# Routed experts: the inner layer handed over in two halves from two banks, and the biases asked for behind the first weights

## The chip, the cores and the metric

One Trainium2 chip, one core of it. The metric is the time of one execution on the device in microseconds (us). The kernel before took 3376.59 us as the median of three runs (3375.28 to 3383.07). PE is the matmul engine (PEld its weight loads), ACT, DVE and POOL are the scalar, vector and GpSimd engines, and SP issues DMAs. PSUM is the accumulator memory, eight banks of 512 float32 values in each of 128 partitions.

## The reference, cut to what matters

Two layers of a graph network, each a graph stage and then a feed-forward stage, over 2500 nodes of 1024 features. The change touches only the last part, the routed experts of the second feed-forward stage (D = 1024, H = 256, E = 8, two experts for each token):

```python
h1 = gelu(einsum('td,edh->teh', flat, rw1) + rb1[None], approximate=False)
expert_out = einsum('teh,ehd->ted', h1, rw2) + rb2[None]
mixed = einsum('ted,te->td', expert_out, weights)      # weights: the two top probabilities, else 0
return (shared_out + mixed).reshape(b, s, d)
```

## The kernel before, in words

The program is a row of stages. The last one, `stage_experts`, is the only one that changes. The stage before it sorts the (token, expert) pairs into 28 groups (PG) of 256 places (GT = 2 tiles of 128 tokens, q = 0 and 1), each group with one expert, and leaves the expert of each group and the token of each place in SBUF. Weights are read again for every group: `raw1` and `raw2` hold 1 MB each, the inner and the outer weights of one expert.

Every float32 product is made of three fast ones: each operand is split into a high part (a copy to the fast format, by ACT) and a low part (the operand less the high part, by DVE), and `split_products` sums high*high, high*low, low*high.

`in_turn(PG, body, 2)` writes the stage out as 30 bodies s = 0 to 29. In body s an engine serves group s (lag 0: loads and splits of weights), group s-1 (lag 1: tokens and inner layer) and group s-2 (lag 2: outer layer and output). Each engine runs its own list in order, and semaphores join the lists. For each body:

- SP (L1979 to L1988) waits until `raw1` has been used and asks for the next inner weights, then the same for `raw2`. Ahead of the loop it asks for the inner biases of all experts (`all_bias1`, two DMAs whose pieces are single values), and in the first turn, behind the weights, for the outer biases (`all_bias2`, 32 KB spread to all 128 partitions, 4 MB written).
- POOL gathers the rows of the two tiles of group s (L1999), and then scatters and adds the output rows of group s-2 into the output (L2009); a scatter waits for that of the group before to have landed.
- PE: transposes of tile 0 of group s-1 into `turned` (L2028, a buffer of two banks that both tiles use in turn), the outer product of tile 0 of group s-2 into `y` (12 matmuls of 512 columns), transposes of tile 1, outer product of tile 1, and then the inner product of group s-1 into `hidden` (48 matmuls of 256 columns: first the 24 of inner features 0 to 127, then the 24 of 128 to 255). Both halves of `hidden` lie in one bank, and one semaphore step says that both are done.
- ACT: copy `hi` of tile 0 and of tile 1 out of `turned` (L2058), high parts of the weights `w1_hi` (L2065) and `w2_hi` (L2068), a small copy of the bias (L2073), the Gelu of both halves of `hidden` (L2079, two instructions), and then the scaling of the two output tiles of group s-2 by their probabilities (L2086).
- DVE: `lo` of tile 0 (L2102), the outer bias added to `y` of tile 0 (L2113), the same for tile 1, low parts of both weights (L1479), and then `h_hi` (L2131) and `h_lo` (L1479) of both halves together.

Transposes of tile 1 wait until `lo` of tile 0 has been made, since they overwrite `turned`. ACT and DVE wait ahead of their first instruction of the stage until all three bias DMAs have landed (`small_in` at 48).

Of the kernel before, what the change touches and what calls it, by code (L numbers as in the profile page):

```python
# [11 lines left out]
P = 128  # L12
# [10 lines left out]
GT = 2  # L23
# [1925 lines left out]
def stage_experts(nc, g):  # L1949
    with ExitStack() as ctx:  # L1950
# [5 lines left out]
        all_bias1, bias1, all_bias2 = sb("all_bias1", [P, EXPERTS * 2]), sb("bias1", [P, 2, 2]), sb("all_bias2", [P, EXPERTS * D])  # L1956
        rows = sb("rows", [P, 2, GT, D])
        hi, lo = sb("hi", [P, KD, GT * P], F32R), sb("lo", [P, KD, GT * P], F32R)
        act_out = sb("act_out", [P, 2 * GT * P])
        h_hi, h_lo = sb("h_hi", [P, 2, GT * P], F32R), sb("h_lo", [P, 2, GT * P], F32R)  # L1960
        y_out = sb("y_out", [P, 2, GT, D])
        turned, y = a.psum("e_turned", [P, 2, HALF]), a.psum("e_y", [P, GT, 2, HALF])
        hidden = a.psum("e_hidden", [P, HALF])
        names = ("small_in raw1_in raw2_in raw1_used raw2_used w1_high w2_high v_done turned_ready "
                 "hi_ready lo_ready hidden_ready act_ready split_ready y_ready y_kept y_scaled bias1_ready").split()
        m = Named(**{n: a.sem(f"e_{n}") for n in names})
        gathered = [[a.sem(f"e_gathered{k}{q}") for q in range(GT)] for k in range(2)]
# [3 lines left out]

        @block.sync
        def _(sp):
            with nc.allow_non_contiguous_dma(reason="two thousand parameters"):
                for c in range(2):
                    sp.dma_start(all_bias1[:].rearrange("p (e m) -> p m e", m=2)[:, c, :],  # L1976
                                 g.rb1.rearrange("e (m p) -> m p e", p=P)[c]).then_inc(m.small_in, 16)

            for i in range(PG):  # L1979
                e = sp.value_load(g.expert[0:1, i:i + 1], min_val=0, max_val=EXPERTS - 1)  # L1980
                at_least(sp, m.raw1_used, i)
                sp.dma_start(raw1[:].rearrange("p (c f) -> p c f", c=KD),
                             g.rw1.rearrange("e (c p) f -> p (e c) f", p=P)[:, bass.ds(e * KD, KD), :]).then_inc(m.raw1_in, 16)
                at_least(sp, m.raw2_used, i)
                sp.dma_start(raw2[:].rearrange("p (m n) -> p m n", m=2),
                             g.rw2.rearrange("e (m p) n -> p (e m) n", p=P)[:, bass.ds(e * 2, 2), :]).then_inc(m.raw2_in, 16)
                if i == 0:
                    sp.dma_start(all_bias2[:], g.rb2.rearrange("e d -> (e d)").partition_broadcast(P)).then_inc(m.small_in, 16)  # L1988

        @block.gpsimd  # L1990
        def _(pool):
# [23 lines left out]
        @block.tensor  # L2015
        def _(pe):
            t = nc.tensor

            def body(item):
                for q in range(GT):  # L2020
                    it = item(1)
                    if it:
                        k = it.i % 2
                        n = it.i * GT + q
                        pe.wait_ge(gathered[k][q], (it.i // 2 + 1) * 16)
                        at_least(pe, m.lo_ready, n)
                        for c in range(KD):
                            tr = t.transpose(turned[:, c // 4, (c % 4) * P:(c % 4 + 1) * P],  # L2028
                                             rows[:, k, q, c * P:(c + 1) * P], g.ident[:])
                        tr.then_inc(m.turned_ready, 1)  # L2030
                    it = item(2)
                    if it:
                        k = it.i % 2
                        pe.wait_ge(m.split_ready, it.i + 1)
                        pe.wait_ge(m.raw2_used, it.i + 1)
                        at_least(pe, m.y_kept, it.i * GT + q - 1)
                        expert_output(t, y[:, q], h_hi, h_lo, w2_hi[:, k], w2_lo[:, k], q).then_inc(m.y_ready, 1)
                it = item(1)
                if it:
                    k = it.i % 2  # L2040
                    pe.wait_ge(m.lo_ready, (it.i + 1) * GT)
                    pe.wait_ge(m.raw1_used, it.i + 1)
                    at_least(pe, m.act_ready, it.i)
                    expert_hidden(t, hidden, w1_hi[:, k], w1_lo[:, k], hi, lo).then_inc(m.hidden_ready, 1)
            in_turn(PG, body, 2)

        @block.scalar
        def _(act):
            s = nc.scalar
            act.wait_ge(m.small_in, 48)  # L2050

            def body(item):
                for q in range(GT):
                    it = item(1)
                    if it:
                        act.wait_ge(m.turned_ready, it.i * GT + q + 1)
                        at_least(act, m.hidden_ready, it.i)
                        s.copy(hi[:, :, q * P:(q + 1) * P],  # L2058
                               turned[:].rearrange("p h (c n) -> p (h c) n", n=P)).then_inc(m.hi_ready, 1)
                it = item(0)  # L2060
                if it:
                    k = it.i % 2
                    act.wait_ge(m.raw1_in, (it.i + 1) * 16)
                    at_least(act, m.hidden_ready, it.i - 1)
# [5 lines left out]
                if it:  # L2070
                    k = it.i % 2
                    e = act.value_load(g.expert[0:1, it.i:it.i + 1], min_val=0, max_val=EXPERTS - 1)
                    s.copy(bias1[:, k, :], all_bias1[:, bass.ds(e * 2, 2)]).then_inc(m.bias1_ready, 1)  # L2073
                    act.wait_ge(m.hidden_ready, it.i + 1)
                    at_least(act, m.split_ready, it.i)
                    act.wait_ge(m.bias1_ready, it.i + 1)
                    for c in range(2):
                        cols = slice(c * GT * P, (c + 1) * GT * P)
                        ins = s.activation(act_out[:, cols], hidden[:, cols], ACT.Gelu, bias=bias1[:, k, c:c + 1])  # L2079
                    ins.then_inc(m.act_ready, 1)  # L2080
                it = item(2)
                if it:
                    for q in range(GT):
# [7 lines left out]
        def _(dve):  # L2091
            v = nc.vector
            st = Steps(dve, m.v_done)
            dve.wait_ge(m.small_in, 48)

            def body(item):
                for q in range(GT):
# [7 lines left out]
                    if it:  # L2105
                        k = it.i % 2
                        n = it.i * GT + q
                        if q == 0:
                            e = dve.value_load(g.expert[0:1, it.i:it.i + 1], min_val=0, max_val=EXPERTS - 1)
                            shift = all_bias2[:, bass.ds(e * D, D)]  # L2110
                        dve.wait_ge(m.y_ready, n + 1)
                        at_least(dve, y_added, (it.i - 1) * GT * 16)
# [3 lines left out]
                if it:  # L2116
# [2 lines left out]
                    dve.wait_ge(m.w1_high, it.i + 1)  # L2119
                    split_vector(v, w1_lo[:, k].rearrange("p c f -> p (c f)"), raw1[:],  # L2120
                                 w1_hi[:, k].rearrange("p c f -> p (c f)"), m.raw1_used)
                    dve.wait_ge(m.raw2_in, (it.i + 1) * 16)
                    dve.wait_ge(m.w2_high, it.i + 1)
                    split_vector(v, w2_lo[:, k].rearrange("p m n -> p (m n)"), raw2[:],
                                 w2_hi[:, k].rearrange("p m n -> p (m n)"), m.raw2_used)
                it = item(1)
                if it:
                    dve.wait_ge(m.act_ready, it.i + 1)
                    at_least(dve, m.y_ready, it.i * GT)
                    whole = act_out[:].rearrange("p (m n) -> p m n", m=2)  # L2130
                    st.link(v.tensor_copy(h_hi[:], whole))  # L2131
                    split_vector(v, h_lo[:], whole, h_hi[:], m.split_ready)
            in_turn(PG, body, 2)


# [100 lines left out]
```

## Time and profile before

| | before |
|---|---|
| median of three runs | 3376.59 us |
| the profiled execution | 3370.22 us, span 3368.4 us |
| mean granted clock of PE | 0.928 |
| busy over the span | PE 87%, DVE 75%, ACT 47%, POOL 49% |
| the experts' stage | from about 2894 us to the end |

Busy shares are means over stages with different limits; the stage of the change is the last 475 us of the span. Times in the rows are counted from the span's start. Matmuls overlap: one of 512 columns has a duration of about 0.40 us, but the next starts about 0.23 us after it, so for PE starts are compared and not durations.

### The profile page before, as it was taken

The page shows a single profiled execution, that of the slowest core. Times are in us where ns is not written, and L with a number is a line of the kernel's source. Part 1 is how long each engine was busy: PE and PEld are TensorE (multiplying, and loading weights), DVE is VectorE, ACT ScalarE, POOL GpSimd, SP SyncE. Part 2 cuts the span into 40 slices and gives each one's busy share as a digit, 9 for nine tenths or more (in the row PEclk, how much of TensorE's full clock was granted, in tenths as well). Part 3 has the DMA queues.
Part 4 walks back from the last instruction along what each step waited for, and adds up shares of the span by engine and source line. Part 5 has one row for each costly group of instructions (what it writes and reads, how often), then busy time and mean ns, then how long its engine had stood idle before and what let it go on. Part 6 is the DMA issues. An engine that isn't in the chain of part 4 may idle for free. (4 is left out here: it accounts for less than half of the span.)

```text
span 3368.4 us, 51550 instructions
## 1 busy us (share of the span) xinstructions
PE 2916.4 (87%) x14130; PEld 2292.0 (68%) x14130; DVE 2530.1 (75%) x5704; ACT 1571.0 (47%) x3051; POOL 1648.1 (49%) x1489
## 2 busy tenths in 40 slices
PE   2988959999997999988888999999995996499996
PEld 1777834444445779777666888888885885388785
DVE  6766859999997673377777999999996654467664
ACT  2545523333334534233333777777774331155553
POOL 2788526666663651677773544444442120033332
PEclk9999979999998985899999999999997887599999
DMA  4433269999991031111112787878875331499997
GB/s 146 121 78 81 71 250 344 350 349 352 348 336 50 25 121 31 28 21 25 24 21 70 251 261 261 261 260 260 263 257 163 113 137 60 162 265 285 283 283 172
DMA packets 218606, 609.65 MB, mean 181 GB/s; under 512 B 41883, under 2 KB 80146, under 8 KB 218334
## 3 DMA queue, kind: packets, MB, share of 16 engines
q0 software_dynamic: 135040, 429.23, 40.6%
q1 hardware_dynamic: 83422, 178.63, 15.4%
q8 instruction: 74, 1.21, 0.1%
q14 instruction: 70, 0.57, 0.1%
HBM read 522.69 MB, written 84.86 MB: 180 GB/s over the span
## 5 line engine op out<-in xcount | busy, mean ns | idle before, releaser
L627 POOL DMA_INDIRECT g_rows<-z_rows,edge_src x704 | 705.9, 1003 | 615.9 <-PE g_totals L1401 307.1
L1064 POOL DMA_INDIRECT shared<-el_rows,edge_src x352 | 336.1, 955 | 172.1 <-issue 107.0
L668 ACT ACTIVATE g_scaled_hi<-g_rows,edge_weight_sorted 128x1024 fp32r<-128x1024 f32 x176 | 202.7, 1151 | 371.2 <-DMA g_rows<-z_rows,edge_src 357.3
L682 PE MATMUL g_sums<-g_rows,g_share 128*128 128x512 f32 x704 | 333.2, 596 | 37.8 <-DMA g_rows<-z_rows,edge_src 37.8
L1394 PE MATMUL g_sums<-g_rows,g_share 128*128 128x256 f32 x1408 | 349.0, 391 | 0.0
L1346 ACT ACTIVATE g_scaled_hi<-g_rows,g_factor 128x256 fp32r<-128x256 f32 x704 | 299.9, 496 | 3.7 <-DMA g_rows<-z_rows,edge_src 1.6
L324 POOL DMA_INDIRECT edge_list<-payload,row_i x196 | 246.6, 1258 | 103.1 <-issue 58.0
L1470 DVE SCALAR_TENSOR_TENSOR g_scaled_lo<-g_rows,g_factor,g_scaled_hi 128x256 fp32r<-128x256 f32 x704 | 293.6, 480 | 1.5 <-ACT g_scaled_hi L1346 1.3
L1394 PEld LDWEIGHTS g_sums<-g_rows,g_share 128*128 128x128 f32 x1408 | 255.6, 192 | 27.6
L1249 DVE TENSOR_REDUCE t_largest<-t_masked 128x4 f32<-128x512 f32 x352 | 231.4, 685 | 49.0 <-PE t_masked L1131 42.5
L703 DVE SCALAR_TENSOR_TENSOR g_scaled_lo<-g_rows,edge_weight_sorted,g_scaled_hi 128x1024 fp32r<-128x1024 f32 x176 | 225.5, 1281 | 48.3 <-ACT g_scaled_hi L668 46.7
L682 PEld LDWEIGHTS g_sums<-g_rows,g_share 128*128 128x128 f32 x704 | 133.7, 190 | 138.7 <-issue 123.4
L2009 POOL DMA_INDIRECT out_dram<-e_y_out,sorted_token x56 | 89.3, 1594 | 271.4 <-ACT e_y_out L2086 256.5
L1432 DVE TENSOR_TENSOR x_all<-x_all,g_sums 128x1024 f32 x176 | 214.0, 1216 | 0.0
L713 DVE TENSOR_TENSOR x_all<-x_all,g_sums 128x1024 f32 x176 | 213.1, 1211 | 0.5 <-PE g_sums L687 0.2
L687 PE MATMUL g_sums<-g_scaled_hi,g_goes 128*128 128x512 f32 x352 | 158.7, 451 | 35.5 <-DVE g_scaled_lo L703 34.9
L687 PEld LDWEIGHTS g_sums<-g_scaled_hi,g_goes 128*128 128x128 f32 x352 | 66.1, 188 | 174.7 <-DVE g_scaled_lo L703 166.6
L1178 ACT ACTIVATE t_apart<-iota,t_minus_place 128x128 fp32r<-128x128 f32 x352 | 125.8, 398 | 105.1 <-PE t_masked L1131 104.2
L1129 PE MATMUL t_masked<-t_never,t_apart 128*128 128x512 f32 x352 | 147.0, 418 | 23.2 <-DVE t_largest L1249 14.5
L1583 POOL TENSOR_TENSOR x_all<-x_all,s_bias 128x1024 f32<-128x1024 f32 (+1 forms) x20 | 46.7, 2356 | 209.1 <-ACT s_rows L1655 209.1
L1479 DVE TENSOR_TENSOR e_w_lo<-e_raw,e_w_hi 128x2048 fp32r<-128x2048 f32 x56 | 125.7, 2285 | 29.2 <-ACT e_w_hi L2065 28.5
L1398 PE MATMUL g_sums<-g_scaled_lo,g_goes 128*128 128x512 f32 x352 | 144.3, 491 | 0.0
(386 smaller groups left out, 8082.4 us busy)
## 6 DMA issues: line engine op xcount, KB each, us to landing
e_raw<-in_L_ffn_rw_dram SPq DMA_DIRECT2D x56, 1024.0 KB, 7.2
g_rows<-z_rows,edge_src POOLq DMA_INDIRECT x704, 5.6
z_rows<-z_zout SPq DMA_DIRECT2D x20, 512.0 KB, 3.1
x_rows<-x_all SPq DMA_DIRECT2D x20, 512.0 KB, 2.6
z_rows<-t_zout SPq DMA_DIRECT2D x20, 512.0 KB, 2.7
s_x<-x_rows SPq DMA_DIRECT2D x10, 1024.0 KB, 8.9
xn_rows<-s_rows SPq DMA_DIRECT2D x10, 1024.0 KB, 4.1
z_x<-in_x_dram SPq DMA_DIRECT2D x19, 512.0 KB
```

Of the source, the lines that this page charges most:

```text
L324: pool.indirect_dma_start(out=g.lists[k], out_offset=bass.IndirectOffsetOnAxis(ap=row_i[0:EP, c:c + 1], axis=0), in_=payload[0:EP, c, :], ...
L627: pool.indirect_dma_start(out=r.rows[:, slot, :], out_offset=None, in_=table, in_offset=bass.IndirectOffsetOnAxis(ap=g.src[:, i * GT + q:i ...
L682: nc.tensor.matmul(sums[:, k, h, :], share[:, k, :], r.rows[:, k * GT, h * HALF:(h + 1) * HALF], start=True, stop=False)
L687: mm = nc.tensor.matmul(sums[:, k, h, :], goes[:, k, :], part[:, m, h * HALF:(h + 1) * HALF], start=False, stop=n == 1)
L703: v.scalar_tensor_tensor(out=scaled_lo[:, m, :], in0=r.rows[:, k * GT + 1, :], scalar=g.weight[:, bass.ds(it.i * GT + 1, 1)], in1=scaled_h ...
L713: v.tensor_tensor(to, to, sums[:, it.buf(4)].rearrange("p h n -> p (h n)"), ALU.add).then_inc(added, 1)
L1064: pool.indirect_dma_start(out=g.edge_el[:, n, :], out_offset=None, in_=g.el, in_offset=bass.IndirectOffsetOnAxis(ap=g.src[:, n:n + 1], axi ...
L1249: v.tensor_reduce(largest[:, q, :], masked[:, n % 3, :].rearrange("p (h n) -> p h n", h=HEADS), AX.X, ALU.max).then_inc(taken, 1)
L1346: ins = s.activation(scaled_hi[:, m, cols], r.rows[:, k * GT + 1, cols], ACT.Copy, scale=factor[:, k, 1, h:h + 1])
L1394: t.matmul(sums[:, m, h // 2, h % 2 * HF:(h % 2 + 1) * HF], share[:, m, h, :], r.rows[:, k * GT, h * HF:(h + 1) * HF], start=False, stop=F ...
L1432: v.tensor_tensor(to, to, sums[:, m].rearrange("p h n -> p (h n)"), ALU.add).then_inc(added, 1)
L1470: ins = v.scalar_tensor_tensor(out=scaled_lo[:, m, cols], in0=r.rows[:, k * GT + 1, cols], scalar=factor[:, k, 1, h:h + 1], in1=scaled_hi[ ...
```

## The change

Four edits, all in `stage_experts`.

1. `hidden` becomes two banks, one for each half of the inner features. PE steps `hidden_ready` after each half. ACT runs the Gelu of a half once that half is done, and DVE splits it once its Gelu is done (`split_hidden`).
2. In DVE's list the split of half 0 stands between the low parts of the inner and of the outer weights, the split of half 1 at the end of the body.
3. PE's outer product waits for half 0 ahead of the products with half 0, and for half 1 ahead of those with half 1. The matmuls, their number and their order stay.
4. The bias DMAs are issued behind the first weights. ACT waits for `bias1_in` ahead of its first bias copy and DVE for `bias2_in` ahead of its first addition of the outer bias; neither waits at the start of the stage.

```diff
-        hidden = a.psum("e_hidden", [P, HALF])
+        hidden = a.psum("e_hidden", [P, 2, HALF])
@@ SP
-            with nc.allow_non_contiguous_dma(reason="two thousand parameters"):
-                for c in range(2):
-                    sp.dma_start(all_bias1[:]..., g.rb1...[c]).then_inc(m.small_in, 16)
             for i in range(PG):
...
                 if i == 0:
-                    sp.dma_start(all_bias2[:], ...).then_inc(m.small_in, 16)
+                    with nc.allow_non_contiguous_dma(reason="two thousand parameters"):
+                        for c in range(2):
+                            sp.dma_start(all_bias1[:]..., g.rb1...[c]).then_inc(m.bias1_in, 16)
+                    sp.dma_start(all_bias2[:], ...).then_inc(m.bias2_in, 16)
@@ PE
+            def output(i, k, q):
+                def h_part(c):
+                    if q == 0:
+                        pe.wait_ge(m.split_ready, 2 * i + c + 1)
+                    return h_hi[:, c, q * P:(q + 1) * P], h_lo[:, c, q * P:(q + 1) * P]
+                for h in range(2):
+                    cols = slice(h * HALF, (h + 1) * HALF)
+                    mm = split_products(t, y[:, q, h, :], h_part, lambda c: (w2_hi[:, k, c, cols], w2_lo[:, k, c, cols]),
+                                        EH // P)
+                mm.then_inc(m.y_ready, 1)
...
-                    pe.wait_ge(m.split_ready, it.i + 1)
...
-                    at_least(pe, m.act_ready, it.i)
-                    expert_hidden(t, hidden, w1_hi[:, k], w1_lo[:, k], hi, lo).then_inc(m.hidden_ready, 1)
+                    for c in range(EH // P):
+                        at_least(pe, m.act_ready, 2 * (it.i - 1) + c + 1)
+                        cols = slice(c * P, (c + 1) * P)
+                        split_products(t, hidden[:, c, 0:GT * P], lambda n: (w1_hi[:, k, n, cols], w1_lo[:, k, n, cols]),
+                                       lambda n: (hi[:, n, :], lo[:, n, :]), KD).then_inc(m.hidden_ready, 1)
@@ ACT
-            act.wait_ge(m.small_in, 48)
...
+                    if it.i == 0:
+                        act.wait_ge(m.bias1_in, 32)
...
-                    act.wait_ge(m.hidden_ready, it.i + 1)
-                    at_least(act, m.split_ready, it.i)
                     for c in range(2):
-                        cols = slice(c * GT * P, (c + 1) * GT * P)
-                        ins = s.activation(act_out[:, cols], hidden[:, cols], ACT.Gelu, bias=bias1[:, k, c:c + 1])
-                    ins.then_inc(m.act_ready, 1)
+                        act.wait_ge(m.hidden_ready, 2 * it.i + c + 1)
+                        at_least(act, m.split_ready, 2 * (it.i - 1) + c + 1)
+                        s.activation(act_out[:, c, :], hidden[:, c, 0:GT * P], ACT.Gelu, bias=bias1[:, k, c:c + 1]).then_inc(m.act_ready, 1)
@@ DVE
-            dve.wait_ge(m.small_in, 48)
+            def split_hidden(i, c):
+                dve.wait_ge(m.act_ready, 2 * i + c + 1)
+                at_least(dve, m.y_ready, i * GT)
+                st.link(v.tensor_copy(h_hi[:, c, :], act_out[:, c, :]))
+                split_vector(v, h_lo[:, c, :], act_out[:, c, :], h_hi[:, c, :], m.split_ready)
...
+                            if it.i == 0:
+                                dve.wait_ge(m.bias2_in, 16)
...
                     split_vector(v, w1_lo..., raw1[:], w1_hi..., m.raw1_used)
+                    split_hidden(it.i, 0)        # of group s-1
...
                     split_vector(v, w2_lo..., raw2[:], w2_hi..., m.raw2_used)
-                    dve.wait_ge(m.act_ready, it.i + 1)
-                    at_least(dve, m.y_ready, it.i * GT)
-                    whole = act_out[:].rearrange("p (m n) -> p m n", m=2)
-                    st.link(v.tensor_copy(h_hi[:], whole))
-                    split_vector(v, h_lo[:], whole, h_hi[:], m.split_ready)
+                    split_hidden(it.i, 1)        # of group s-1
```

## Rows read from the trace of the kernel before

**Rows 1.** Stages: window, length, five engines' busy, clock, DMA share, GB/s.
```profile
2960.00:3040.00 80.00, 73.45 (x479) 64.79 (x478) 56.37 (x44) 47.86 (x49) 27.16 (x22) 1.00 0.99 280
...
2896.00:2918.00 22.00, 1.97 (x8) 1.57 (x8) 0.00 (x0) 0.00 (x0) 2.73 (x3) 0.50 0.99 381
```
**Rows 2.** Chain of waits, last stage: start us, us, what.
```profile
2896.98 21.71 DMA e_all_bias<-in_L_ffn_rb_dram
...
3121.19 8.00 DMA out_dram<-e_y_out,sorted_token
3129.23 4.67 issue
```
**Rows 3.** Timeline of PE over one body: start us, us, what, idle before.
```profile
3107.47 1.06 PE L2028 MATMUL e_turned<-ident,e_rows 128*128 128x128 f32 x8
...
3116.80 0.28 PE L165 MATMUL e_hidden<-e_hi,e_w_lo 128*128 128x256 f32 x1
3116.92 1.04 PE L2028 MATMUL e_turned<-ident,e_rows 128*128 128x128 f32 x8
3119.20 0.50 PE L165 MATMUL e_y<-e_w_hi,e_h_hi 128*128 128x512 f32 x1 [1.24 <-DVE e_h_lo L1479]
...
3121.88 0.40 PE L165 MATMUL e_y<-e_w_hi,e_h_lo 128*128 128x512 f32 x1
3122.34 1.06 PE L2028 MATMUL e_turned<-ident,e_rows 128*128 128x128 f32 x8
...
3126.04 0.28 PE L165 MATMUL e_hidden<-e_hi,e_w_hi 128*128 128x256 f32 x1
```
**Rows 4.** Timeline of ACT over the same body.
```profile
3117.12 0.84 ACT L2079 ACTIVATE e_act_out<-e_hidden,e_bias 128x256 f32<-128x256 f32 x2 [3.69 <-PE e_hidden L165]
3117.85 2.19 ACT L2086 ACTIVATE e_y_out<-e_y_out,sorted_prob 128x1024 f32<-128x1024 f32 x2
3119.93 1.01 ACT L2058 CAST e_hi<-e_turned 128x1024 fp32r<-128x1024 f32 x1
...
3126.29 1.92 ACT L2068 CAST e_w_hi<-e_raw 128x2048 fp32r<-128x2048 f32 x1
3128.11 0.19 ACT L2073 COPY e_bias<-e_all_bias 128x2 f32 x1
```
**Rows 5.** Timeline of DVE over the same body.
```profile
3117.99 0.43 DVE L2131 CAST e_h_hi<-e_act_out 128x512 fp32r<-128x512 f32 x1 [1.00 <-ACT e_act_out L2079]
3118.45 0.69 DVE L1479 TENSOR_TENSOR e_h_lo<-e_act_out,e_h_hi 128x512 fp32r<-128x512 f32 x1
3120.97 1.22 DVE L2102 TENSOR_TENSOR e_lo<-e_turned,e_hi 128x1024 fp32r<-128x1024 f32 x1 [1.83 <-ACT e_hi L2058]
...
3127.38 4.49 DVE L1479 TENSOR_TENSOR e_w_lo<-e_raw,e_w_hi 128x2048 fp32r<-128x2048 f32 x2
```
**Rows 6.** The line that asks for the outer weights (L1985), 2960 to 3325.
```profile
DMA to landing us min/median/max: 6.9/7.6/9.2
```
**Rows 7.** Timeline of SP at the start of the stage.
```profile
2893.87 1.02 SPq L1976 DMA_DIRECT2D e_all_bias<-in_L_ffn_rb_dram  x2
...
2896.51 0.43 SPq L1985 DMA_DIRECT2D e_raw<-in_L_ffn_rw_dram  x1
```
**Rows 8.** The outer weights' first request (L1985), by itself.
```profile
DMA to landing us min/median/max: 12.5/12.5/12.5
```
**Rows 9.** Timeline of ACT at the start of the stage.
```profile
2920.52 1.89 ACT L2068 CAST e_w_hi<-e_raw 128x2048 fp32r<-128x2048 f32 x1
...
2934.48 1.28 ACT L2079 ACT_TABLE_LOAD   x1
```
**Rows 10.** Timeline of DVE at the start of the stage.
```profile
2920.75 4.49 DVE L1479 TENSOR_TENSOR e_w_lo<-e_raw,e_w_hi 128x2048 fp32r<-128x2048 f32 x2 [27.84 <-ACT e_w_hi L2065]
```
**Rows 11.** Timeline of PE at the start of the stage.
```profile
2930.82 0.58 PE L165 MATMUL e_hidden<-e_hi,e_w_hi 128*128 128x256 f32 x1 [2.36 <-DVE e_lo L2102]
...
2938.70 1.04 PE L2028 MATMUL e_turned<-ident,e_rows 128*128 128x128 f32 x8
...
2943.89 1.03 PE L2028 MATMUL e_turned<-ident,e_rows 128*128 128x128 f32 x8
```

More of the change, by code:

```diff
@@ L1958, in stage_experts @@
         hi, lo = sb("hi", [P, KD, GT * P], F32R), sb("lo", [P, KD, GT * P], F32R)
-        act_out = sb("act_out", [P, 2 * GT * P])
+        act_out = sb("act_out", [P, 2, GT * P])
         h_hi, h_lo = sb("h_hi", [P, 2, GT * P], F32R), sb("h_lo", [P, 2, GT * P], F32R)
@@ L1962, in stage_experts @@
         turned, y = a.psum("e_turned", [P, 2, HALF]), a.psum("e_y", [P, GT, 2, HALF])
-        hidden = a.psum("e_hidden", [P, HALF])
-        names = ("small_in raw1_in raw2_in raw1_used raw2_used w1_high w2_high v_done turned_ready "
+        hidden = a.psum("e_hidden", [P, 2, HALF])
+        names = ("bias1_in bias2_in raw1_in raw2_in raw1_used raw2_used w1_high w2_high v_done turned_ready "
                  "hi_ready lo_ready hidden_ready act_ready split_ready y_ready y_kept y_scaled bias1_ready").split()
@@ L1973, in _ @@
         def _(sp):
-            with nc.allow_non_contiguous_dma(reason="two thousand parameters"):
-                for c in range(2):
-                    sp.dma_start(all_bias1[:].rearrange("p (e m) -> p m e", m=2)[:, c, :],
-                                 g.rb1.rearrange("e (m p) -> m p e", p=P)[c]).then_inc(m.small_in, 16)
             for i in range(PG):
@@ L1987, in _ @@
                 if i == 0:
-                    sp.dma_start(all_bias2[:], g.rb2.rearrange("e d -> (e d)").partition_broadcast(P)).then_inc(m.small_in, 16)
+                    with nc.allow_non_contiguous_dma(reason="two thousand parameters"):
+                        for c in range(2):
+                            sp.dma_start(all_bias1[:].rearrange("p (e m) -> p m e", m=2)[:, c, :],
+                                         g.rb1.rearrange("e (m p) -> m p e", p=P)[c]).then_inc(m.bias1_in, 16)
+                    sp.dma_start(all_bias2[:], g.rb2.rearrange("e d -> (e d)").partition_broadcast(P)).then_inc(m.bias2_in, 16)
         @block.gpsimd
@@ L2033, in body @@
                         k = it.i % 2
-                        pe.wait_ge(m.split_ready, it.i + 1)
                         pe.wait_ge(m.raw2_used, it.i + 1)
                         at_least(pe, m.y_kept, it.i * GT + q - 1)
-                        expert_output(t, y[:, q], h_hi, h_lo, w2_hi[:, k], w2_lo[:, k], q).then_inc(m.y_ready, 1)
+                        output(it.i, k, q)
                 it = item(1)
@@ L2056, in body @@
                         act.wait_ge(m.turned_ready, it.i * GT + q + 1)
-                        at_least(act, m.hidden_ready, it.i)
+                        at_least(act, m.hidden_ready, 2 * it.i)
                         s.copy(hi[:, :, q * P:(q + 1) * P],
@@ L2063, in body @@
                     act.wait_ge(m.raw1_in, (it.i + 1) * 16)
-                    at_least(act, m.hidden_ready, it.i - 1)
+                    at_least(act, m.hidden_ready, 2 * (it.i - 1))
                     s.copy(w1_hi[:, k].rearrange("p c f -> p (c f)"), raw1[:]).then_inc(m.w1_high, 1)
@@ L2121, in body @@
                                  w1_hi[:, k].rearrange("p c f -> p (c f)"), m.raw1_used)
+                it = item(1)
+                if it:
+                    split_hidden(it.i, 0)
+                it = item(0)
+                if it:
+                    k = it.i % 2
                     dve.wait_ge(m.raw2_in, (it.i + 1) * 16)
```

## The prediction, made before the changed kernel ran

> **What bounds the kernel now.** I read the busy times by stage first, then the chain of waits, then one body of the stage engine by engine. Only the last 475 us of the span matter here, since no other stage changes. In the middle of that stage PE is busy 73.45 of 80 us at full clock and the DMA share is 0.99 [rows 1]; both could be the bound. The chain of waits is nearly all scatter-adds, but each is followed by some 4 us of "issue", in which no transfer is waited for: the scatter had landed at 3129.19 and the next one started at 3134 [rows 2]. So the chain names a companion and not the bound.
>
> The timelines give the loop. From the transposes of tile 1 at 3107.47 to the same at 3122.34 a body takes 14.87 us [rows 3]; 26 bodies repeat it. PE's only hole of size is the 1.24 us ahead of the outer product of tile 0, which waits for `h_lo`. There is a second, smaller one: the last matmul of that product starts at 3121.88, the next instruction could start 0.23 us later, but the transposes of tile 1 start at 3122.34. They wait for `lo` of tile 0, which ends at 3120.97 + 1.22 = 3122.19 [rows 5]. And that `lo` hangs on a chain which starts where the inner product ends (3116.92): 0.20 us, two Gelus (0.73 us from start to the next start), two output scalings (2.08), `hi` (1.04), `lo` (1.22), 0.15 us of signal [rows 4, 5]. The sum is 5.42 us, just 3122.34 - 3116.92. Two chains thus end within 0.23 us of each other at the transposes of tile 1, and the change shortens mainly one.
>
> **The steady bodies, part by part.**
>
> Two banks, Gelu by halves. The Gelu of half 0 goes out of the way: its half is done 24 matmuls before the end, 2.88 us earlier at the spacing of 0.12 us, when ACT is idle (it waits 3.69 us there) [rows 4]. Behind the end of the inner product one Gelu is left: 0.37 us of start-to-start (half of 0.73) goes. Everything behind it on ACT, scalings, `hi`, and through it `lo` and the transposes of tile 1, moves by 0.37.
>
> The wait for `h_lo`. Half 1 now needs Gelu until 3117.59, then a copy and a subtraction of 256 columns. The trace has neither shape. The halves of 0.43 and 0.69 are the lower ends, the whole durations the upper ones [rows 5]; I take 0.29 and 0.43, near the halves, since 2048, 1024 and 512 columns took 2.28, 1.22 and 0.69, which leaves 0.16 us that doesn't shrink. With the links that is 0.75 us, so half 1 is ready at about 3118.4. PE finds half 0 ready at 3117.74 and works 0.70 us on three matmuls with it, then goes on. The outer product of tile 0 ends about 1.4 us earlier. This is the large gain that one would read from the hole of 1.24, and it is worth nothing: the transposes of tile 1 stand right behind it and wait for `lo` of tile 0, now at 3121.97. The hole moves 3 us down PE's list and is 1.1 us wide there. So a body gains 0.37, not 1.24 nor 1.47, and takes 14.50 us.
>
> The other edits on this path. Waits that are satisfied cost nothing visible: the inner product follows the outer one behind three such waits at the ordinary spacing. I take 0 for the new ones, 0.1 at most for the one between the halves of the inner product, 2.6 us in all; for a gain there is no reason. On DVE the split of half 0 stands ahead of the outer weights' low part. It adds 0.75 us there: `w1_lo` ends at 3129.67, the Gelu of half 0 at 3129.6 in that body, the split ends at 3130.4, `w2_lo` at 3132.7, the split of half 1 at 3133.5. That is 1.7 us behind the end of the inner product, and PE needs it only 2.9 us behind it (5.05 less nine matmuls of 0.233). Covered with 1.2 us to spare. The signal that frees `raw2` comes 0.8 us later as well. SP's only queue behind it is the next `raw1`, which waits longer anyway. The outer weights, asked for at 3117.17 and landed 7.6 us later (9.2 at most) [rows 6], were used at 3126.29: of 9.1 us there remain 9.1 - 0.8 - 0.37 = 7.95. A late landing delays `w2_hi` by up to 1.3 us, which ACT's idle time ahead of the Gelus takes.
>
> Count: the transposes of tile 1 of bodies 3 to 28, and once more the last Gelu ahead of the final scatters: 27 x 0.37 = 10.0 us.
>
> **The start of the stage.** Before, ACT's first copy waited for the broadcast bias, asked for at 2896.98 and landed 21.71 us later [rows 2]; the weights had landed long before. Now both weights are asked for 1.0 us earlier (the two bias issues in front took 1.02), the outer ones at 2895.5, and land 12.5 us later, at 2908.0 [rows 7, 8]. `w2_hi` starts there and not at 2920.52 [rows 9], and `w2_lo` ends at 2908.0 + 1.9 + 2.3 = 2912.2 and not at 2920.75 + 4.49 = 2925.24 [rows 10]: 13.0 us earlier. The inner product of group 0 follows it at 2917.8 and ends at 2925.7 (it was 2930.82 to 2938.70, at a clock that rose on the way) [rows 11].
>
> But what is late next stands behind it in ACT's list: the Gelu comes after `w1_hi` and `w2_hi` of group 1, and their DMAs, issued at 2908.7 and 2912.4, queue behind the 4 MB of bias on the same queue. The order in that queue shows in the rows: 0.5 us after the inner weights come the outer ones, landing after 12.5 us, and the bias last, with 381 GB/s flowing to the end [rows 1, 2, 8]. The total in front of the bias hasn't changed, so it lands at about 2918.2 again; then 3.15 MB (two weights, two gathers) at 381 GB/s take 8.3 us, with landing 2926.7. From there: `w2_hi` 1.9, bias copy and table load 1.6 [rows 9], Gelu of half 0 0.5, split 0.75, `w2_lo` 2.3, split of half 1 0.75, nine matmuls 2.1: transposes of tile 1 at 2936.6 instead of 2943.89 [rows 11], 7.3 us earlier. The later bodies take this over whole. Here the new place of `w2_lo`, between the two splits, does cost: 2.3 us of PE waiting. Bounds: 14.4 us if the weights of group 1 don't queue (13.0, and the 1.4 of body 2), downwards, the inner bias' single-value pieces now stand in front of the broadcast: they had at most the 2.1 us from 2893.87 to the window from 2896, whose 22 us at 381 GB/s are all the other 8.4 MB; and PE, which now idles from 2926 to 2931, may be back at its lower level, as it was at 0.50 when idle at 2896 to 2918 [rows 1]: nine matmuls and the transposes would take 1.9 us more. 7.3 - 2.1 - 1.9 = 3.3. I take 7.3, since the queue's order is in the rows and the 2.1 is an upper bound of which some is latency.
>
> On that landing the Trainium skill ("DMA: Bandwidth & Descriptors", Specifications) gives a fabric ceiling of 435 GB/s, which this window's 381 doesn't reach; at the ceiling the landing would be some 3 us earlier and the stage's start would gain about 10. A second page speaks against me: "TensorE: Matmul & The Clock Gate" ("What's actually happening") says that an idle PE falls back to its lower clock; by that the gain would be 5.4. Whether the new idle time is long enough for it no row shows.
>
> **Sum.** 7.3 + 10.0 = 17.3 us off the profiled 3370.22 us (span 3368.4 and 1.8 around it) gives 3352.9. That execution was 6.4 us under the median of the runs shown; against the median, 3376.6 - 17.3 = 3359.3, which I give.
>
> **The rivals.**
> - DMA is the bound. For: share 0.99. Against: the 4 us of slack behind each scatter, and 0.4 us of 14.87 is less than what a share counted over waiting packets can tell. Bodies stay at 14.87, only the start gains: 3376.6 - 7.3 = 3369.3. Chance 0.12.
> - The start gains nothing, or 3 at most, as the weights of group 1 come as late as the first ones did: 3376.6 - 10 - 1.5 = 3365. Chance 0.09.
> - PE regains its whole hole, because scalings or `hi` aren't in the way as I read them: 27 x 1.47 + 7.3 = 47 off, 3330. Chance 0.05; the chain of 5.42 us closes to 0.01.
> - Slower: a new ring. `w2_hi` (1.94), bias copy (0.25), Gelu 0 (0.5), split 0 (0.75), `w2_lo` (2.29), reissue (0.2), landing: 5.9 us and the landing. It is under 14.50 while a landing takes less than 8.6; the median 7.6 passes, and the request now falls nearer to the scatters. At 9.2 in every body: 15.13, +0.26 x 26 - 7.3, about 0. At 10, beyond the maximum in [rows 6]: 15.9, +27.6 - 7.3, 3397. It decides from a mean of 9.6 up, where the loss passes 10 us. Chance 0.08.
> - The change does nothing that can be measured (both parts hidden by something that I don't see): within 5 us of 3376. Chance 0.06.
> - My forecast: 0.60, itself from 3352 to 3367.
>
> **How the numbers follow.** A change under 0.3%, 10 us, can't be told here. Faster holds nearly all of the forecast (0.55), the full regain 0.05, and some of the first two rivals 0.08: 0.68. Slower 0.08, same 0.24. Range: 3346 to 3373, which takes in the first two rivals, the upper bound at the start and 0.3% of scatter, and leaves out the regain, the slow ring, and part of the null case.
>
> **What would show it.** Right: the body is 14.50 us from transposes to transposes; PE's idle time stands ahead of the transposes of tile 1 (1.1 us, released by `lo`) and not ahead of the outer product; only one Gelu follows the end of the inner product; ACT's first copy starts near 2904 and the first Gelu near 2930, behind `w2_hi`. Wrong: a hole of PE still ahead of the outer product, released by `h_lo` of half 1; landings of the outer weights over 8.6 us with ACT waiting for them; a first Gelu that waits for the bias.

## The result

| | before | changed |
|---|---|---|
| median of seven runs | 3379.5 us | 3366.33 us |
| profiled execution | 3370.22 us, span 3368.4 | 3362.09 us, span 3360.3 |
| from the first gather of the stage to the end | 473.8 us | 460.5 us |
| of it to the transposes of tile 1 in body 2 | 49.3 us | 45.8 us |
| and from there to the end | 424.5 us | 414.7 us |
| a body in the middle | 14.87 us | 14.51 us |

The ratio is 0.9964 (0.9952 to 0.9976): 12 to 13 us less, and the interval leaves 1 out. Forecast were 17.3 us less, 3359.3 us, with a range of 3346 to 3373. Of the 7.0 us by which 3366.3 lies above 3359.3, 2.9 come from the kernel before alone, whose median is 3379.5 us over seven runs and was 3376.6 over the three that the forecast started from. The bodies gave the forecast 10 us (9.8). The start gave 3.5 us where 7.3 were forecast. The profiled spans differ by only 8.1 us because the stage began 5.2 us later in this execution (first gather at 2899.81, before at 2894.59) for reasons ahead of the change; so from here on the start is measured from the first gather.

One body of the changed kernel, PE's timeline (start us, us, what, idle before). It answers to [rows 3]:

```profile
3105.41 1.06 PE L2038 MATMUL e_turned<-ident,e_rows 128*128 128x128 f32 x8 [1.12 <-DVE e_lo L2118]
...
3114.87 1.03 PE L2038 MATMUL e_turned<-ident,e_rows 128*128 128x128 f32 x8
3115.66 0.47 PE L165 MATMUL e_y<-e_w_hi,e_h_hi 128*128 128x512 f32 x1
...
3118.40 0.39 PE L165 MATMUL e_y<-e_w_hi,e_h_lo 128*128 128x512 f32 x1
3119.92 1.06 PE L2038 MATMUL e_turned<-ident,e_rows 128*128 128x128 f32 x8 [1.14 <-DVE e_lo L2118]
```

The outer product follows the transposes of tile 0 at once; the hole of 1.24 us is gone. It stands 3 us later, 1.14 us wide, ahead of the transposes of tile 1, and its releaser is `lo`. From one to the next of these transposes it is 3119.92 - 3105.41 = 14.51 us.

ACT over the same body, answering to [rows 4]:

```profile
3112.24 0.48 ACT L2091 ACTIVATE e_act_out<-e_hidden,e_bias 128x256 f32<-128x256 f32 x1 [0.87 <-ACT e_bias L2086]
3115.07 0.47 ACT L2091 ACTIVATE e_act_out<-e_hidden,e_bias 128x256 f32<-128x256 f32 x1 [2.35 <-PE e_hidden L165]
3115.44 2.18 ACT L2097 ACTIVATE e_y_out<-e_y_out,sorted_prob 128x1024 f32<-128x1024 f32 x2
3117.52 1.00 ACT L2069 CAST e_hi<-e_turned 128x1024 fp32r<-128x1024 f32 x1
```

One Gelu lies 2.8 us ahead of the other. Behind the end of the inner product (3114.87) come 0.20 us, one Gelu (0.37 to the next start), two scalings (2.08), `hi`: the same chain as before without 0.37.

DVE, answering to [rows 5]:

```profile
3112.75 0.29 DVE L2109 CAST e_h_hi<-e_act_out 128x256 fp32r<-128x256 f32 x1
3113.08 0.43 DVE L1479 TENSOR_TENSOR e_h_lo<-e_act_out,e_h_hi 128x256 fp32r<-128x256 f32 x1
3113.42 2.28 DVE L1479 TENSOR_TENSOR e_w_lo<-e_raw,e_w_hi 128x2048 fp32r<-128x2048 f32 x1
3115.62 0.29 DVE L2109 CAST e_h_hi<-e_act_out 128x256 fp32r<-128x256 f32 x1
```

The two shapes that the trace before didn't have took 0.29 and 0.43 us, as estimated.

The start of the stage, SP (answers to [rows 7]):

```profile
2900.05 0.41 SPq L1977 DMA_DIRECT2D e_raw<-in_L_ffn_rw_dram  x1
2900.66 0.42 SPq L1980 DMA_DIRECT2D e_raw<-in_L_ffn_rw_dram  x1
2901.12 7.73 SPq L1985 DMA_DIRECT2D e_all_bias<-in_L_ffn_rb_dram  x2
2908.90 5.09 SPq L1987 DMA_DIRECT2D e_all_bias<-in_L_ffn_rb_dram  x1
2914.75 0.38 SPq L1977 DMA_DIRECT2D e_raw<-in_L_ffn_rw_dram  x1
2918.56 3.58 SPq L1980 DMA_DIRECT2D e_raw<-in_L_ffn_rw_dram  x1
```

The two requests of single values, 1.02 us of SP's time in front of the weights, take 7.73 us behind them; the broadcast behind those takes 5.09 us (0.77 before) and is only asked for at 2914. The outer weights of group 1 take 3.58. The single values also cost transfer time. Two windows, ahead of them and while most of their pieces move (columns as in [rows 1]):

```profile
2908.00:2911.80 3.80, 1.25 (x6) 0.84 (x4) 1.01 (x1) 1.90 (x1) 0.00 (x0) 0.50 1.02 408
2911.80:2915.80 4.00, 0.00 (x0) 0.00 (x0) 1.28 (x1) 1.71 (x1) 0.00 (x0) 0.50 0.86 227
```

ACT and PE at the start (answer to [rows 9] and [rows 11]):

```profile
2908.78 1.90 ACT L2076 CAST e_w_hi<-e_raw 128x2048 fp32r<-128x2048 f32 x1 [61.10 <-DMA e_raw<-in_L_ffn_rw_dram]
2914.09 1.90 ACT L2079 CAST e_w_hi<-e_raw 128x2048 fp32r<-128x2048 f32 x1 [3.41 <-DMA e_raw<-in_L_ffn_rw_dram]
...
2931.59 1.92 ACT L2076 CAST e_w_hi<-e_raw 128x2048 fp32r<-128x2048 f32 x1 [8.94 <-DMA e_raw<-in_L_ffn_rw_dram]
2934.11 1.90 ACT L2079 CAST e_w_hi<-e_raw 128x2048 fp32r<-128x2048 f32 x1 [0.60 <-DMA e_raw<-in_L_ffn_rw_dram]
```

```profile
2938.82 0.77 PE L165 MATMUL e_y<-e_w_hi,e_h_hi 128*128 128x512 f32 x1 [5.84 <-DVE e_h_lo L1479]
...
2941.59 0.79 PE L165 MATMUL e_y<-e_w_hi,e_h_hi 128*128 128x512 f32 x1 [1.15 <-DVE e_h_lo L1479]
2942.19 0.63 PE L165 MATMUL e_y<-e_w_lo,e_h_hi 128*128 128x512 f32 x1
2942.61 0.63 PE L165 MATMUL e_y<-e_w_hi,e_h_lo 128*128 128x512 f32 x1
```

And windows of the changed kernel (columns as in [rows 1]):

```profile
2934.00:2938.80 4.80, 0.00 (x0) 0.01 (x1) 2.75 (x4) 4.66 (x6) 0.00 (x0) 0.67 0.31 63
2941.60:2944.00 2.40, 2.40 (x6) 1.92 (x7) 1.07 (x1) 0.00 (x0) 0.00 (x0) 0.50 0.77 215
```

As forecast the first Gelu waits for `w2_hi` of group 1, and the copies for the weights' landing (8.94 us ahead of `w1_hi`, 0.60 more ahead of `w2_hi`). PE is idle for 5.84 us, in which its granted clock falls, waits again 1.15 us in the middle of its first outer product (for `w2_lo` between the two splits), and works at 0.50 of its clock: the 512-column matmuls start every 0.43 us and not every 0.23.

### The profile page after: what moved, and what is told of

Its sections match the earlier page's. It is cut to its first block and busy times, and to the rows that moved or that the text cites. A ratio compares the mean times of both kernels' runs of the same rounds, so it can differ in the third digit from the quotient of the medians.

```text
span 3360.3 us, 51659 instructions
## 1 busy us (share of the span) xinstructions
PE 2922.5 (87%) x14130; PEld 2295.0 (68%) x14130; DVE 2535.8 (75%) x5760; ACT 1574.5 (47%) x3051; POOL 1649.2 (49%) x1489
## 5 line engine op out<-in xcount | busy, mean ns | idle before, releaser
L1249 DVE TENSOR_REDUCE t_largest<-t_masked 128x4 f32<-128x512 f32 x352 | 231.8, 685 | 51.4 <-PE t_masked L1131 44.5
L1479 DVE TENSOR_TENSOR e_w_lo<-e_raw,e_w_hi 128x2048 fp32r<-128x2048 f32 x56 | 127.9, 2284 | 25.4 <-ACT e_w_hi L2076 22.4
```

Source lines behind the costliest of these rows:

```text
L1249: v.tensor_reduce(largest[:, q, :], masked[:, n % 3, :].rearrange("p (h n) -> p h n", h=HEADS), AX.X, ALU.max).then_inc(taken, 1)
```

## The experiments

Twelve kernels, in three groups of four; kernels of a group shared a chip and the runs of the kernel before. On the chip of the second group every kernel took some 440 us longer in stages ahead of this one (before: 3819.43 us); bodies of the changed kernel's form (split_first) take 14.52 us there as well, and only ratios of a group are compared. "Start" is the time from the first gather to the transposes of tile 1 in body 2, "rest" from there to the end, both from one profiled execution of each kernel.

| kernel | ratio to before, interval | start | rest | median body |
|---|---|---|---|---|
| before | | 49.3 | 424.5 | 14.88 |
| changed | 0.9964 (0.9952 to 0.9976) | 45.8 | 414.7 | 14.52 |
| halves | 0.9973 (0.9959 to 0.9986) | 49.6 | 415.0 | 14.52 |
| biases | 0.9988 (0.9978 to 0.9998) | 43.5 | 424.2 | 14.88 |
| bias1_first | 0.9958 (0.9944 to 0.9973) | 43.1 | 414.6 | 14.52 |
| bias2_late | 0.9935 (0.9921 to 0.9950) | 36.8 | 414.7 | 14.52 |
| scale_early | 0.9944 (0.9927 to 0.9961) | 45.9 | 411.0 | 14.04 |
| scale_w2first | 0.9954 (0.9940 to 0.9969) | 44.5 | 414.2 | 14.26 |
| before_scale_early | 1.0017 (1.0006 to 1.0028) | 49.6 | 428.2 | 14.63 |
| split_first | one run | 43.1 | 414.8 | 14.52 |
| changed_half_weights | one run | 39.7 | 415.4 | 14.52 |
| early_half_weights | one run | 42.8 | 380.5 | 13.20 |
| bias2_late_scale_late | 0.9956 (0.9940 to 0.9972) | 36.6 | 424.6 | 14.63 |
| bias2_late_scale_early | 0.9934 (0.9916 to 0.9951) | 37.0 | 412.8 | 14.50 |

### halves: the split into halves alone

```diff
 # the changed kernel, but
+            act.wait_ge(m.bias1_in, 32); act.wait_ge(m.bias2_in, 16)   # at the start of ACT and of DVE
-                    if it.i == 0: act.wait_ge(m.bias1_in, 32)
 # and the two inner-bias DMAs ahead of the first weights
```

> The kernel before with the split into halves alone (two banks, two Gelus, two splits); the biases are asked for and waited for as before. My theory: a body takes 14.51 us and not 14.87, so 27 x 0.37 = 10.0 us, and body 2 gains its hole of 1.24 us as a whole (nothing stands behind it there but a short chain): 11.3 us less than before. Rival 1 (the bodies gain nothing by the halves, the time comes from the start): within 2 us of before. Rival 2 (the low part of the outer weights between the two splits costs in every body): 14.6 us or more a body, under 7 us in all.

9.1 us less by the ratio (0.0027 x 3377), where 11.3 were expected. The bodies are as expected, the rest 9.5 us shorter. Body 2 gained nothing (start 49.6), against the 1.24 us expected of it. Its hole changed its place only: the first Gelu comes late, since the table load of 1.28 us stands behind the wait for half 0, `w2_lo` follows the split of half 0 on DVE, and half 1 has to wait for it.

```profile
2941.80 1.28 ACT L2092 ACT_TABLE_LOAD   x1 [1.55 <-PE e_hidden L165]
2943.09 0.47 ACT L2092 ACTIVATE e_act_out<-e_hidden,e_bias 128x256 f32<-128x256 f32 x1
```

```profile
2944.27 2.28 DVE L1479 TENSOR_TENSOR e_w_lo<-e_raw,e_w_hi 128x2048 fp32r<-128x2048 f32 x1
2946.47 0.29 DVE L2112 CAST e_h_hi<-e_act_out 128x256 fp32r<-128x256 f32 x1
```

### biases: the requests alone

```diff
 # the kernel before, but the bias DMAs behind the first weights, and
-            act.wait_ge(m.small_in, 48)          # and the same on DVE
+                    if it.i == 0: act.wait_ge(m.bias1_in, 32)
+                            if it.i == 0: dve.wait_ge(m.bias2_in, 16)
```

> The kernel before with the bias requests alone moved behind the first weights and waited for where they are used; Gelu and split in one piece as before. My theory now, after the trace of the changed kernel: the first Gelu is held by the outer weights of group 1, which queue behind the biases. A body stays at 14.87 us. The start gains some 4.4 us, a little more than the 3.3 of the changed kernel, because here the low part of the outer weights stands ahead of the whole split and not between two halves of it (PE doesn't wait 1.15 us in the middle of its first outer product). Rival (my forecast's figure for the start): 7.3 us. Rival (the start is worth nothing, the rest hides it): within 1 us of before.

The start is 5.8 us shorter, the body unchanged; 4.1 us by the ratio (0.7 to 7.4). It is more than the 3.5 of the changed kernel, as expected, because DVE's order doesn't hold the first outer product, and more than the 4.4 expected: the clock rose within that product, and its last five matmuls start every 0.23 us, not every 0.43, which is 1.0 us. The two parts add up to the whole only roughly (9.1 + 4.1 = 13.2), and at the start they hinder one another.

### bias1_first: the single values back in front

```diff
+            for c in range(2): sp.dma_start(all_bias1..., g.rb1...[c]).then_inc(m.bias1_in, 16)   # ahead of the loop
             for i in range(PG):
...
-                        for c in range(2): sp.dma_start(all_bias1..., ...)                        # in turn 0
```

> The changed kernel with the two inner-bias DMAs (single values) back ahead of the first weights, their counting apart kept. Theory: behind the weights these two requests hold SP for 7.73 us and the next one for 5.09 us (before: 1.02 and 0.77), and their pieces hold the queue. In front they cost SP about 1 us. The outer weights of group 1 are then asked for without SP being held, and land about 2 us earlier relative to the first gather: 2 us less than the changed kernel, 15 less than before. Rival: the 4 MB broadcast alone holds the weights of group 1, and where the small pieces stand makes no difference: the same as the changed kernel, within 1 us at the start of the stage.

```profile
2900.77 1.02 SPq L1976 DMA_DIRECT2D e_all_bias<-in_L_ffn_rb_dram  x2
...
2903.89 0.64 SPq L1988 DMA_DIRECT2D e_all_bias<-in_L_ffn_rb_dram  x1
```

SP is free again after 0.64 us behind the broadcast. `w2_hi` of group 1 starts 32.1 us behind the first gather (34.3 in the changed kernel), the start is 2.7 us shorter. So the place of the 2048 single values did cost, 2.2 us of these 2.7; the nine matmuls behind PE's wait give the rest (3.57 us, 4.01 in the changed kernel), since the clock rose three matmuls before their end.

### bias2_late: the broadcast behind the weights of group 1

```diff
 # bias1_first, and
-                if i == 0:
+                if i == 1:
                     sp.dma_start(all_bias2[:], ...).then_inc(m.bias2_in, 16)
```

> As bias1_first, and the 4 MB broadcast asked for one turn later, behind the weights of group 1. Theory: the weights of group 1 land some 10 us earlier, the first Gelu follows the end of the first inner product at once, and what is left at the start is weights, splits and the inner product at the low clock. The transposes of tile 1 of body 2 come about 36 us behind the first gather (before 49.3, the changed kernel 46.0): 23 us less than before in all. Rival (ACT's own order holds the first Gelu, not the queue): the same as bias1_first. Rival (the broadcast is now late for the first bias addition and PE waits for that): under 5 us gained on bias1_first.

```profile
2920.24 1.91 ACT L2077 CAST e_w_hi<-e_raw 128x2048 fp32r<-128x2048 f32 x1
2922.05 1.90 ACT L2080 CAST e_w_hi<-e_raw 128x2048 fp32r<-128x2048 f32 x1
2923.84 0.19 ACT L2087 COPY e_bias<-e_all_bias 128x2 f32 x1
2926.68 1.28 ACT L2092 ACT_TABLE_LOAD   x1 [2.64 <-PE e_hidden L165]
```

ACT no longer waits for the weights of group 1; the first Gelu waits for PE. (Those of group 2 now follow the broadcast, and ACT waits 0.50 and 1.82 us for them.) The start is 12.5 us shorter than before (36.8, about 36 expected), the whole 22 us by the ratio. The granted clock rose at 2926 and stayed at 1.00; up to 3320 PE's longest idle time behind that is 1.4 us and no longer 5.84. This shows the queue: the broadcast, not ACT's order by itself, held the first Gelu.

### scale_early and scale_w2first: the other chain taken away

```diff
+            def scale_out(item): ...                     # the two output scalings of group s-2
                     for c in range(2):
+                        if c == 1:
+                            scale_out(item)
                         act.wait_ge(m.hidden_ready, 2 * it.i + c + 1)
...
-                it = item(2)                             # the scalings at the end of the body
 # scale_w2first also: on DVE, split_hidden(it.i, 0) behind the low part of the outer weights
```

> The changed kernel with the two output scalings of ACT moved ahead of the Gelu of half 1, into its idle time there (2.35 us; they take 2.08). Theory of the chain (the transposes of tile 1 wait for lo of tile 0, hi of tile 0, two scalings, one Gelu): hi follows the transposes of tile 0 at once, PE's hole of 1.14 us goes, and a body takes 14.51 - 1.29 = 13.22 us, 33 us less than the changed kernel. Rival 1 (the ring of the outer weights: w2_hi, bias copy, Gelu 0, split 0, w2_lo, request, landing, 5.9 us and the landing): at a landing of 7.6 us 13.5 us a body, at 8.3 us 14.2; ACT then waits for DMA ahead of w2_hi. Rival 2 (the DMA engines are the bound, share 0.99): the body stays at 14.2 to 14.5 us whatever the order, and landings grow.

> As scale_early, and DVE's split of half 0 back behind the low part of the outer weights, which opens the ring. Theory of the ring: if scale_early stays above 13.22 us a body because of the ring, this one comes to 13.2 to 13.4 us. Theory of DMA as the bound: no difference to scale_early, with gathers or weights waited for in both. If scale_early is at 13.22 already, the same or up to 0.3 us a body more, since the halves are then ready 0.1 to 0.3 us too late for PE.

Both theories had something right. The shortest bodies of scale_early take 13.2 us, as the chain says. But the median is 14.04, seven of those behind the first take over 15 us and the longest 19.2; the rest is 3.9 us shorter than in split_first on the same chip, of 33 expected. The ring isn't the cause: with it open the bodies are no shorter (14.26). Among the waits of scale_early, 3400 to 3760 us (waiting for whom: us in total, times, longest), two now name DMA, weights and gathered rows; in the changed kernel's middle (2960 to 3310) such waits of ACT and PE come to 0.3 us in all:

```profile
ACT e_w_hi L2088 <- DMA e_raw<-in_L_ffn_rw_dram: 37.2, 14, 5.8
DVE e_lo L2124 <- ACT e_hi L2078: 30.8, 40, 1.7
DVE e_h_hi L2115 <- ACT e_act_out L2102: 25.5, 13, 5.0
PEld e_turned L2038 <- DMA e_rows<-xn_rows,sorted_token: 20.2, 18, 2.7
```

The gathers' landings took 8.6/9.8/11.7 us (minimum, median, maximum) against 6.7/7.4/8.9 in the changed kernel, and 6.8/7.8/9.5 in split_first on the same chip.

### before_scale_early: the scalings alone

```diff
 # the kernel before, with scale_out(item) ahead of both Gelus
```

> The kernel before with the scalings alone moved ahead of the Gelus. Theory of two chains that end within 0.23 us of each other: here the other chain is left, PE's hole of 1.24 us ahead of the outer product stays and the one of 0.23 ahead of the transposes of tile 1 goes, so a body takes 5.19 + 3.70 + 5.75 = 14.64 us and the kernel 26 x 0.23 = 6 us less than before. Either edit alone is worth little (10 and 6 us), both together 43. Rival (the scalings alone are the bound): 1.3 us a body or more, 33 us.

The undisturbed body is 14.62 us, as the two chains say (14.64). Expected were 6 us less; the kernel is 6.5 us slower (1.0006 to 1.0028), the rest in the profile 3.7 us longer: eleven bodies take 0.2 to 3.7 us more, and the scatters' landings took 9.7/11.0/13.3 us where before they took 7.4/8.3/9.0. An edit that shortens the chain by 0.23 us moved a group's first scatter some 3 us ahead, from 2.35 us behind the end of the inner product to 0.70 us ahead of it (medians), into the weights' transfers and beside DVE's low parts. POOL itself takes longer there, 2.46 us for a group's first scatter where it took 1.61:

```profile
3505.17 2.46 POOL L2009 DMA_INDIRECT out_dram<-e_y_out,sorted_token  x1 [8.44 <-ACT e_y_out L2058]
3507.94 1.59 POOL L2009 DMA_INDIRECT out_dram<-e_y_out,sorted_token  x1 [0.30 <-issue]
```

### split_first: DVE's order in body 1

```diff
                     split_hidden(it.i, 0)
+                    if it.i == 0: split_hidden(it.i, 1)     # ahead of w2_lo, for group 0
```

> The changed kernel with both halves of the first group split ahead of the low part of the outer weights, in body 1 alone. Theory: PE's wait of 1.15 us in the middle of the first outer product goes, the transposes of tile 1 of body 2 come 44.6 us behind the first gather and not 45.8, at the same low clock (matmuls of 512 columns start every 0.43 us). Rival (something else holds PE there too): 45.8.

43.1, 2.7 us less; more than the 1.2 expected. PE's wait went (no gap between the third and the fourth matmul, both 0.43 us apart as the others), and the clock rose in the middle of the same product: its last five matmuls start every 0.23 us and not every 0.43, which is 1.0 us more.

### changed_half_weights and early_half_weights: is it the bytes?

```diff
+                n1, n2 = (KD, 2) if i == 0 else (KD // 2, 1)
-                sp.dma_start(raw1[...], g.rw1...[:, bass.ds(e * KD, KD), :])
+                sp.dma_start(raw1[...][:, 0:n1, :], g.rw1...[:, bass.ds(e * KD, n1), :])   # raw2 alike, n2 of 2
```

> The changed kernel, but from group 1 on only half of each weight tensor is read from memory (1 MB a body in place of 2 MB; the other half keeps what group 0 left there); all computation stays in form. Theory of the chain (hidden end, Gelu, two scalings, hi, lo): a body takes 14.51 us as with all the bytes, 414.7 us from the transposes of tile 1 of body 2 to the end. Theory that the changed kernel is already held by the DMA engines (about 290 GB/s, share 1.00): bodies get shorter, towards 13.5 us.

> scale_early with the same half of the weight bytes left out. Theory that the DMA engines hold scale_early (4.2 MB a body at 290 GB/s are 14.4 us): now every body takes 13.2 us, without the longer ones of 15 to 19 us, landings of gathers fall below 8 us, and the stage is 33 us shorter than in the changed kernel. Rival (the earlier scatters themselves hold gathers and weights, whatever the bytes): bodies still between 13.2 and 19 us, mean above 14.

The windows of the middle, first the changed kernel with half the weights, then scale_early with half the weights:

```profile
2960.00:3310.00 350.00, 322.67 (x2121) 284.92 (x2120) 253.85 (x242) 211.47 (x218) 124.77 (x98) 1.00 0.87 218
```

```profile
2960.00:3290.00 330.00, 328.16 (x2185) 295.53 (x2185) 264.50 (x249) 219.30 (x225) 162.81 (x100) 1.00 0.92 235
```

The pair decides it for the changed kernel. With the chain in place, a quarter of the stage's bytes less changes nothing: 14.52 us a body. With the chain gone the same bytes less give 13.20 us in 21 of 27 bodies, 34 us less rest than the changed kernel, the 33 that scale_early should have given. (The gathers' landings stay above the 8 us expected: 8.3.) So the changed kernel is bound by its chain, but by a hair. Over 3400 to 3760 us on one chip split_first, whose bodies are those of the changed kernel, moved 285 GB/s, and scale_early, freed of the chain, 285 as well: the next 1.3 us of chain bring 3.9 us in all, and the rest of the 33 came only with fewer bytes. early_half_weights also keeps the early scatters and POOL's long issues (3.17 us in most bodies), so neither of these by itself makes the long bodies.

### bias2_late with the scalings late, and early

```diff
 # scale_late: bias2_late, and the scalings of group s-3 behind hi of tile 0
                     if q == 0:
                         scale_out(item(3))
```

> bias2_late, and the two output scalings moved the other way: into the next body, behind hi of tile 0. The chain loses them as in scale_early (13.2 us a body if nothing else holds), but the scatters come about 1 us later in the body than in the changed kernel and not 2.4 us earlier. Theory of DMA capacity: the mean body is 14.3 to 14.5 us all the same, and the kernel takes what bias2_late takes or up to 5 us less, 22 to 27 us less than before. Theory of phase (only the early scatters hurt): a body of 13.2 to 13.8 us, 40 us or more less than before.

> bias2_late and scale_early together. The start gains 12.5 us as in bias2_late, the bodies the 4 us that scale_early got beside the changed kernel: 26 us less than before. If it is held by the DMA engines, ACT waits for weights and PE for gathered rows in the longer bodies as it did there.

Late scalings lose 10 us of rest against bias2_late, where 0 to 5 us less or 40 us less were expected. POOL issues its gathers behind the scatters, these now come later (first scatter 3.47 us behind the end of the inner product, 1.99 in bias2_late), and PE waits for the gathered rows in every body though they take no longer to land (7.7 us, 7.9 in bias2_late). Waits of PE, 2960 to 3310:

```profile
PE e_turned L2039 <- DMA e_rows<-xn_rows,sorted_token: 34.7, 24, 2.7
```

So capacity isn't the whole of it; the place of the gathers counts as well. Early scalings on bias2_late give 0.9934, the same as bias2_late alone (0.9935; the intervals all but coincide), and not the 26 us less that were expected. bias2_late, with less changed, is the version to keep: it beats both kernels, 22 us under before and, by the ratios to it, some 10 us under the changed one.

## Why the prediction was right, and where not

The bodies, step by step. The chain of 5.42 us without half of the Gelus: measured 5.05 (3119.92 - 3114.87), forecast 5.05. The body 14.51, forecast 14.50. The hole 1.14 us wide and released by `lo`, forecast 1.1. The splits 0.29 and 0.43, forecast the same. The new waits on PE cost nothing between the halves of the inner product (5.76 us for 48 matmuls in both kernels). The ring: the outer weights land 5.7 us after their request (4.9 to 7.3), less than before (7.6); they are now asked for 3.0 us behind the inner ones and not 2.2, which may be the reason, but no run takes that apart. ACT never waited for them in the middle. 27 x 0.37 = 10.0, measured 9.8. halves confirms it by itself.

The start: the mechanism was right, the size of two terms wrong. The step "landing 2926.7" is 32.1 us behind the first gather; measured 34.3 (2934.09 less 2899.81). Missing were the 2.2 us that the single values cost when they stand behind the weights. I had them as an upper bound of 2.1 in the range, just too low, and left them out of the sum; bias1_first puts them back in front and hits 32.1. That hit is in part luck: the sum has the broadcast landed at 2918.2, where the row gives 2896.98 + 21.71 = 2918.69, and from there the same working ends at 2927.0, 32.4 behind the first gather. Second, "nine matmuls 2.1": 4.0 us, as PE had idled 5.84 us and ran at 0.50 of its clock. That, too, stood in the prediction only as a bound (1.9). 7.3 - 2.2 - 1.9 = 3.2, measured 3.5. Both were asymmetric: each could only cost. With two such terms the lower end was the better estimate, and the sum would have been 13.3 us; the median difference is 13.2.

On the two pages of the Trainium skill: "TensorE: Matmul & The Clock Gate" ("What's actually happening"), which says that an idle PE falls back to its lower clock, was right here, 0.50 after 5.84 us without work, and its sum (5.4 at the start) was nearer than mine. The ceiling that the Trainium skill gives in "DMA: Bandwidth & Descriptors" (Specifications, 435 GB/s) was no guide: the windows with weights, gathers and scatter-adds mixed moved 278 to 290 GB/s at a share of 0.98 to 1.01, and no kernel with all the bytes moved more there.

The rivals. "DMA is the bound" was wrong for this change and mostly right for the next one; changed_half_weights rejects it, early_half_weights shows how near it was. "PE regains its whole hole" was rejected by the chain, as the trace said. The slow ring didn't come, and opening it in scale_early (scale_w2first) made no body shorter. "The start gains nothing, or 3 at most" was nearly right in size (3.5) and right in its mechanism, which my forecast shared; its 11.5 us less in all lies nearer to the measured 12 to 13 than my 17.3.

## What to carry to other kernels

A hole on the busiest engine isn't worth its width: look for what the next instruction behind it waits for, and add up that second chain to its end; here they lay 0.23 us apart, and of 1.24 us only 0.37 came. Requests that only have to be early enough belong behind everything that the first steps need, counted by the queue and not by the program: here the 4 MB one turn later shortened the start by 6.3 us (43.1 to 36.8), where the changed place of all the requests had given 3.5. Before an edit that moves transfers, halve the bytes in a trial run, before it and with it: the pair tells whether a chain or the transfers hold the loop.

## What was not expected of the hardware

- Two DMA requests of 1024 single values took SP 1.02 us with nothing ahead of them and 7.73 to 7.92 us behind 2 MB of weights, and held SP's next request for 4.6 to 5.1 us (changed, biases, split_first).
- Scatter-adds that start 2.4 to 3.1 us earlier in the body, among the weights' transfers, land in 10.4 to 11.0 us and not in 7.8 to 8.3, while 278 to 286 GB/s flow (before_scale_early, scale_early, scale_w2first). The gathers behind them land in 9.8 to 10.2 us (the latter two) and not in 7.4 to 7.8 (changed, split_first).
- POOL's issue of a scatter took 1.56 to 1.64 us in the kernel before and in the changed one, where no subtraction of DVE's L1479 overlaps it. In scale_early all 25 first scatters of a group overlap one and take 1.76 to 3.17 us; 14 of them end 1.49 us behind the end of a low part of weights, the other 11 end 0.82 us behind the end of `h_lo` of half 0. In before_scale_early it is up to 3.75 us, 1.5 us behind such an end again. The fixed distance points to DVE's subtraction as what POOL waits for; no run takes it away.
- The experts' stage of split_first, the changed kernel but for body 1, kept its 14.52 us a body on a chip where the stages ahead took 440 us longer.
